# Attention with six score banks dealt out anew, exponentials head by head, and row sums once per pair of heads

## The chip, the cores and the metric

One core of one Trainium2 chip runs the whole layer. The metric is device time in microseconds (us) of one execution.

## The reference

The layer is causal attention, a residual and a layer norm, then a routed feed-forward (32 experts, one expert for each token, a bound on tokens per expert), a residual and a layer norm. The change is in the attention, and in where the work that follows a batch's attention is placed. Shapes: 8 batches of 1024 tokens, width 256, 16 heads of 64, keys and values from a latent of width 64, all float32.

```python
q_blhd = jnp.einsum('bld,dhk->blhk', x_bld, Wq)
latent_bll = jnp.einsum('bld,dc->blc', x_bld, Wkv_down)
k_blhd = jnp.einsum('blc,chk->blhk', latent_bll, Wk_up)
v_blhd = jnp.einsum('blc,chk->blhk', latent_bll, Wv_up)
attn = jnp.einsum('bqhd,bkhd->bhqk', q_blhd, k_blhd) / jnp.sqrt(HD)
attn = softmax(where(causal_mask, attn, neg_inf), axis=-1)
y_blhd = jnp.einsum('bhqk,bkhd->bqhd', attn, v_blhd)
out = jnp.einsum('bqhd,hdo->bqo', y_blhd, Wout)
x = _layernorm(x + out)
```

## The kernel before

**Pairs and slots.** Heads are taken two at a time: 8 batches of 8 pairs, 64 pairs; below, "pair p" is the place 0 to 7 in its batch. For each pair the kernel computes scores with keys on the partitions ("turned" scores) in 12 slots t (`NSLOT`, `SLOT`). Slots 0 to 3 are the first 512 queries against key blocks 0 to 3, slots 4 to 11 the second 512 queries against key blocks 0 to 7. The causal mask cuts the queries per head to 384 in slots 1 and 9, 256 in slots 2 and 10, and 128 in slots 3 and 11; the other six have 512.

**What a slot does.** TensorE (PE) forms the scores of both heads in `turned_scores`: for each head a product with the high parts (L669) and one with the low parts and the row maxima (L672). Slot n uses the two-bank tensor `turned_ps[n % 2]`, one bank per head. ScalarE (ACT) takes the exponential of both heads in one instruction (L928) into one of six buffers `probs`. GpSimd (POOL) clears what lies past the diagonal in slots 0 to 3 and 8 to 11 (`keep_past`, L451) and adds the exponentials up over the slots (`add_probs`, L466 to L475). PE multiplies the exponentials with the values (`values`, L692), two slots at a time, in the even slots: in slot t those of t-2 and t-1. ACT copies the result out (`copy_heads`).

**Row maxima.** The maxima for the next pair come from a second set of scores, with queries on the partitions: 24 units per pair, two in each slot (`row_scores`, L645), into two banks `row_ps`. VectorE (DVE) takes the maximum (`row_max`, L1078 and L1082). `turn_max` (L655) transposes them, `copy_max` (L1093) copies them out, and SyncE (SP) loads them into `q_max` with a DMA.

**Row sums.** `total` (L702) multiplies the added exponentials with ones, once for the first 512 queries (slot 6) and once for the second (slot 4 of the next pair). Each use has one product per head, and each product fills 64 rows of the bank. A float32 product is two instructions in the trace. DVE transposes the bank (`invert`, L1099), takes the reciprocal and transposes back (`invert_rows`, L1106 and L1111), and POOL divides the heads' outputs (`divide`, L483).

**The single bank `misc_ps`.** Everything else of PE goes through it, in the order of `LATE[gp, t]` (and `EARLY`, which runs between scores and row units): maxima to transpose, sums, queries of later pairs (`q`, L593), the output projection of the batch before (`proj`, L711), its transposes (`x1T`), router logits (`logits`) and the counts of places (`pos`). Each use waits until the one before was read. Every engine walks through the slots in the same order. In pairs 0 to 2 of a batch the batch before is projected, normalised and routed; POOL's part of the layer norm is `roots` (L489 to L501), and POOL sends the tokens away in pairs 4 and 5 (`send`, L508). Pairs 6 and 7 prepare the next batch. After the last pair comes `ENDING`, which finishes the last batch, and then the experts.

## Time and profile before

| what | us |
|---|---|
| median of three runs (2668.49 to 2669.42) | 2668.54 |
| profiled execution, its own time | 2669.0 |
| its span, first to last instruction | 2666.9 |
| PE busy | 2466.4 (92% of the span) |
| POOL busy | 1674.7 (63%) |
| DVE busy | 1532.1 (57%) |
| ACT busy | 994.5 (37%) |

The attention of the 64 pairs runs from 53.5 to 2327 us; the experts follow. Busy time is time in which an instruction runs, and matmuls overlap: the distance between the starts of two neighbours is what the first one costs. The mean granted TensorE clock is 0.968 of 2.4 GHz.

### The profile page before, as it was taken

To read this page: it belongs to the slowest core of one execution; us is meant where nothing else is said; L and a number is where in the kernel's file an instruction comes from. 1 tells how busy PE (TensorE), PEld (TensorE's weight loads), DVE (VectorE), ACT (ScalarE), POOL (GpSimd) and SP (SyncE) were. 2 spreads that over 40 slices of the span, in tenths; PEclk is the share of its full clock that TensorE was granted. 3 is DMA by queue.
4 is the path that set the end of the run, shared out by engine and by line. 5 is a ranking of instruction groups with operands and counts; after the bars stand their busy time and mean duration, and the time that the engine had idled before them with its cause. 6 is when DMAs were issued, how large, how long until landed. Compare 5 with 4: busy or idle time off the path is not lost.

```text
span 2666.9 us, 35643 instructions
## 1 busy us (share of the span) xinstructions
PE 2466.4 (92%) x12040; PEld 1578.6 (59%) x12040; DVE 1532.1 (57%) x4298; ACT 994.5 (37%) x1480; POOL 1674.7 (63%) x1623
## 2 busy tenths in 40 slices
PE   6999999999999999999999999999999999959995
PEld 5555665556655665566555655566556655646663
DVE  3666556665666556655666476656665666235453
ACT  3344424442444334433444244433443344212222
POOL 0677656865687657766686468665876678523343
PEclk7999999999999999999999999999999999969998
DMA  2122100200011001100020002000110011233552
GB/s 82 57 66 71 37 10 16 68 17 13 15 52 31 13 13 40 40 17 13 17 66 18 9 17 64 17 17 9 44 41 13 17 32 33 64 106 126 167 169 67
DMA packets 96804, 118.88 MB, mean 45 GB/s; under 512 B 12288, under 2 KB 75782, under 8 KB 96624
## 3 DMA queue, kind: packets, MB, share of 16 engines
q1 hardware_dynamic: 89712, 99.98, 13.4%
q0 software_dynamic: 6912, 16.64, 1.8%
q8 instruction: 97, 1.59, 0.3%
q14 instruction: 83, 0.68, 0.1%
HBM read 46.91 MB, written 37.90 MB: 32 GB/s over the span
## 4 chain that ended last, share of the span: by engine, by line
PE 62%; POOL 17%; issue 11%; DVE 6%; ACT 2%; DMA 1%; POOLq 0%; SPq 0%; ACTq 0%; DVEq 0%
PE value_ps L692 14%; POOL sums L475 10%; PE turned_ps L669 9%; PE row_ps L645 7%; PE turned_ps L672 7%; PE misc_ps L593 6%; PE misc_ps L711 4%; PE turned_ps L857 4%; PE misc_ps L702 4%; POOL probs L451 2%; POOL slots_x L508 2%; DVE masked_row L1078 1%; ACT probs L928 1%; PE misc_ps L876 1%; PE value_ps L876 1%
## 5 line engine op out<-in xcount | busy, mean ns | idle before, releaser
L928 ACT ACTIVATE probs<-turned_ps 128x1024 f32<-128x1024 f32 (+3 forms) x768 | 616.9, 811 | 961.2 <-PE turned_ps L672 953.1
L475 POOL TENSOR_TENSOR sums<-sums,probs 128x1024 f32<-128x1024 f32 (+3 forms) x512 | 830.6, 1622 | 23.1 <-ACT probs L928 14.7
L1078 DVE CUSTOM_DVE_ANT_0 masked_row<-row_ps,future 128x384 bf16<-128x384 f32 (+3 forms) x1024 | 464.4, 489 | 406.2 <-PE row_ps L645 405.1
L692 PE MATMUL value_ps<-probs,lat_keys 128*64 128x512 f32 (+3 forms) x3072 | 607.5, 508 | 44.8 <-POOL probs L451 41.2
L669 PE MATMUL turned_ps<-q_hl,lat_hi 128*128 128x512 f32 (+3 forms) x1536 | 570.3, 379 | 1.5 <-ACT fold_v L974 1.5
L672 PE MATMUL turned_ps<-q_max,lat_lo 65*128 65x512 f32 (+3 forms) x1536 | 528.4, 352 | 2.6 <-DMA q_max<-max_rows 2.6
L451 POOL TENSOR_SCALAR_AFFINE_SELECT probs<-probs 128x256 f32<-128x256 f32 x512 | 210.3, 411 | 500.3 <-ACT probs L928 499.6
L645 PE MATMUL row_ps<-lat_hi,q_hl 128*128 128x512 f32 (+3 forms) x1536 | 452.8, 366 | 14.3 <-DVE unit_max L1078 7.3
L471 POOL TENSOR_TENSOR sums<-probs 128x768 f32<-128x768 f32 (+1 forms) x128 | 268.5, 2097 | 233.0 <-ACT probs L928 233.0
L669 PEld LDWEIGHTS turned_ps<-q_hl,lat_hi 128*128 128x128 f32 x1536 | 294.2, 192 | 197.3 <-issue 149.0
L692 PEld LDWEIGHTS value_ps<-probs,lat_keys 128*64 128x64 f32 x3072 | 180.7, 137 | 348.5 <-issue 222.4
L1082 DVE TENSOR_REDUCE unit_max<-row_ps 128x1 f32<-128x512 f32 x512 | 327.9, 681 | 41.2 <-PE row_ps L645 36.4
L645 PEld LDWEIGHTS row_ps<-lat_hi,q_hl 128*128 128x128 f32 x1536 | 277.0, 193 | 91.2 <-DVE unit_max L1078 45.3
L672 PEld LDWEIGHTS turned_ps<-q_max,lat_lo 65*128 65x128 f32 x1536 | 295.4, 192 | 30.8 <-DMA q_max<-max_rows 2.9
L711 PE MATMUL misc_ps<-fold_v,headsT 128*128 128x256 f32 x1008 | 232.9, 384 | 2.4 <-POOL headsT L483 2.2
L711 PEld LDWEIGHTS misc_ps<-fold_v,headsT 128*128 128x128 f32 x1008 | 190.0, 192 | 35.1 <-issue 8.7
L1099 DVE STREAM_TRANSPOSE sums_cols<-misc_ps 128x512 f32<-128x512 f32 x127 | 91.1, 717 | 147.2 <-PE misc_ps L702 147.2
L483 POOL TENSOR_TENSOR headsT<-headsT,rinv_rows 128x512 f32<-128x512 f32 x128 | 164.2, 1283 | 1.9 <-DVE rinv_rows L1111 1.9
L910 ACT CAST q_hl<-misc_ps 64x512 fp32r<-64x512 f32 x125 | 72.6, 581 | 234.3 <-PE misc_ps L593 234.3
L857 PE MATMUL turned_ps<-ex_xT,ex_w 128*128 128x320 f32 x512 | 146.7, 440 | 0.0
L702 PE MATMUL misc_ps<-sums,ones_f 128*64 128x512 f32 x508 | 131.3, 595 | 7.7 <-DVE max_rows L1093 7.2
L1135 DVE TENSOR_TENSOR x<-misc_ps,x_in 128x256 f32<-128x256 f32 x64 | 27.2, 425 | 165.1 <-PE misc_ps L711 165.1
(187 smaller groups left out, 2317.4 us busy)
## 6 DMA issues: line engine op xcount, KB each, us to landing
q_max<-q_hl SPq DMA_DIRECT2D x256, 128.0 KB
slots_x<-zero_rows SPq DMA_DIRECT2D x8, 1290.0 KB, 6.4
ex_x<-slots_x SPq DMA_DIRECT2D x64, 129.0 KB, 3.5
x_in<-in_L_attn_x_bld SPq DMA_DIRECT2D x8, 1024.0 KB, 6.0
layer_out<-x_in SPq DMA_DIRECT2D x8, 1024.0 KB, 5.0
ex_w<-in_L_ffn_w_gate SPq DMA_DIRECT2D x32, 256.0 KB, 3.7
ex_w<-in_L_ffn_w_up SPq DMA_DIRECT2D x32, 256.0 KB, 3.8
ex_w<-in_L_ffn_w_down SPq DMA_DIRECT2D x32, 256.0 KB, 4.0
```

Source lines behind the costliest of these rows:

```text
L451: nc.gpsimd.affine_select(out=block, in_=block, pattern=[[0, 2], [1, P]], compare_op=ALU.is_ge, fill=0.0, base=0, channel_multiplier=-1).t ...
L471: nc.gpsimd.tensor_tensor(sums[c][:, :, q0:BANK], before[:, :, q0:BANK], now[:, :, q0:BANK], ALU.add).then_inc(added, 1)
L475: nc.gpsimd.tensor_tensor(sums[c][:, :, q0:BANK], sums[c][:, :, q0:BANK], now[:, :, q0:BANK], ALU.add).then_inc(added, 1)
L645: nc.tensor.matmul(dst[:, 0:k1 - k0], q_hl[gp % 2][:, h, i * P:(i + 1) * P], lat_hi[b % 2][:, k0:k1], start=True, stop=True).then_inc(rows ...
L669: nc.tensor.matmul(dst, lat_hi[b % 2][:, keys], q_hl[gp % 2][:, h, cols], start=True, stop=False)
L672: mm = nc.tensor.matmul(dst, lat_lo[b % 2][:, keys], q_max[:, c, h, q0:BANK], start=False, stop=True)
L692: mm = nc.tensor.matmul(value_ps[h * LD:(h + 1) * LD, q0:BANK], lat_keys[b % 2][:, j, :], probs[:, n % NPROBS, h, q0:BANK], start=(j == 0) ...
L711: mm = nc.tensor.matmul(bank[:, 0:D], headsT[:, (NPAIR * b + j) % NHEADS, i * P:(i + 1) * P], fold_v[:, j, :], start=(j == 0), stop=(j == ...
L857: mm = nc.tensor.matmul(turned_ps[f][:, m, 0:C], ex_w[e % AHEAD][:, m, kd, f * P:(f + 1) * P], ex_xT[:, g % 2, kd, u * C:(u + 1) * C], sta ...
L928: nc.scalar.activation(probs[:, n % NPROBS, :, q0:BANK], turned_ps[n % 2][:, :, q0:BANK], ACT.Exp).then_inc(exp_done, 1)
L1078: nc.vector.tensor_tensor_reduce(masked_row[n % 2][:, 0:width], row_ps[n % 2][:, 0:width], future[:, BANK - width:], scale=-1.0, scalar=-M ...
L1082: nc.vector.tensor_reduce(dst, row_ps[n % 2][:, 0:width], AX.X, ALU.max, negate=True).then_inc(max_done, 1)
```

## The change

- **Banks.** The six banks of the two kinds of scores are dealt out as three single banks for the turned scores (`SCORE_BANKS`) and three for the row units (`ROW_BANKS`).
- **Exponentials.** Each head's scores have a bank and an exponential of their own in the eight wide slots. In the narrow slots (2, 3, 10, 11) both heads share one bank, one product of each kind, and one exponential.
- **Row sums.** `sums` runs once per pair, in slot 4 of the next pair: four products (two heads, two halves of the queries), each filling 32 rows of the bank. DVE transposes the bank once, and in slots 6 and 8 takes the reciprocals of a half, with two small copies to fill all rows, and transposes them. There are three buffers of sums instead of two.
- **Order.** The maxima of the next pair's first half are transposed in slot 6 instead of within slot 4. `divide` moves to slots 7 and 0, and one half is divided a pair later. The projection, the layer norm and the routing of the batch before move to later slots. In the last pair all eight projections stand in slots 9 to 11.
- Some buffers share memory: `wkv2` with `sums_cols`, `zero_rows` with the router's.

`LAG` is 0, so the lines with it change nothing.

```diff
+        half_sums = [sb(f"half_sums{i}", [P, 2, BANK], F32, attn) for i in range(3)]
+        sums_of = lambda gp, c: half_sums[2 if c else gp % 2]
+        SCORE_BANKS = [turned_ps[0][:, 0, :], turned_ps[0][:, 1, :], turned_ps[1][:, 0, :]]
+        ROW_BANKS = [row_ps[0][:, :], row_ps[1][:, :], turned_ps[1][:, 1, :]]
+        BANKS_OF = [1 if 2 * (BANK - first_query(t)) <= BANK else 2 for t in range(NSLOT)]
...
             if gp + 1 < PAIRS:
                 late[1].append(("q", gp + 1, 1))
-                EARLY[gp, 4] = [("maxT", gp + 1, 0)]
+                late[6].append(("maxT", gp + 1, 0))
             if gp:
-                late[4].append(("sums", gp - 1, 1))
-            late[6].append(("sums", gp, 0))
+                late[4].append(("sums", gp - 1))
             if gp + 2 < PAIRS:
-                late[9 if p == NPAIR - 2 else 8].append(("q", gp + 2, 0))
+                late[9 if p == NPAIR - 2 else 7 if b and p < 2 else 8].append(("q", gp + 2, 0))
             if b and p == 0:
-                for i, t in enumerate((3, 5, 7, 10, 11)):
+                for i, t in enumerate((9, 10, 11)):
                     late[t].append(("proj", b - 1, i))
             if b and p == 1:
-                for i, t in enumerate((3, 5, 7)):
-                    late[t].append(("proj", b - 1, 5 + i))
-                for kd in range(KD):
-                    late[10 + kd].append(("x1T", b - 1, 0, kd))
+                for i, t in enumerate((3, 5, 9, 10, 11)):
+                    late[t].append(("proj", b - 1, 3 + i))
             if b and p == 2:
-                for kd in range(KD):
-                    late[3 + 2 * kd].append(("x1T", b - 1, 1, kd))
-                late[7].append(("logits", b - 1))
+                for use, t in zip([(hf, kd) for hf in range(2) for kd in range(KD)], (3, 5, 7, 10)):
+                    late[t].append(("x1T", b - 1, *use))
+                late[11].append(("logits", b - 1))
             if b and p == 3:
-                late[3].append(("pos", b - 1))
+                late[7].append(("pos", b - 1))
...
-        for t, i in zip((1, 2, 3, 5, 7, 8, 9, 10), range(NT)):
+        for t, i in zip((9, 9, 10, 10, 11, 11, 11, 11), range(NT)):
             LATE[PAIRS - 1, t].append(("proj", LAST, i))
...
POOL:
-                    if gp and t == 0:
+                    if gp >= 2 and t == 0:
+                        divide(gp - 2, 1)
+                    if gp and t == 7:
                         divide(gp - 1, 0)
-                    if gp and t == 6:
+                    if gp == PAIRS - 1 and t == 9:
                         divide(gp - 1, 1)
-                    if b and (p, t) in ((1, 0), (2, 0)):
+                    if b and (p, t) in ((1, 8), (2, 2)):
                         roots(b - 1, p - 1)
...
PE, row_scores:
                 if n >= 2:
-                    pe.wait_ge(max_done, n - 1)
+                    if n in ROW_BEFORE:
+                        pe.wait_ge(max_done, ROW_BEFORE[n] + 1)
-                dst = row_ps[n % 2]
+                dst = ROW_BANKS[row_bank(n)]
PE, turned_scores:
-                for h in range(2):
-                    dst = turned_ps[n % 2][:, h, q0:BANK]
-                    nc.tensor.matmul(dst, lat_hi[b % 2][:, keys], q_hl[gp % 2][:, h, cols], start=True, stop=False)
+                for h in range(BANKS_OF[t]):
+                    m = scored(n - 1) + h
+                    if m >= 3:
+                        pe.wait_ge(exp_done, m - 2)
+                    heads = slice(0, 2) if in_one_bank(t) else h
+                    nc.tensor.matmul(scores_of(n, h), lat_hi[b % 2][:, keys], q_hl[gp % 2][:, heads, cols], start=True, stop=False)
...
PE, total:
                 for h in range(2):
-                    mm = nc.tensor.matmul(bank[h * LD:(h + 1) * LD, :], ones_f[:, :], sums[c][:, h, :], start=True, stop=True)
+                    for c in range(2):
+                        k = 2 * h + c
+                        mm = nc.tensor.matmul(bank[k * 32:(k + 1) * 32, :], ones_f[:, :], sums_of(gp, c)[:, h, :],
+                                              start=True, stop=True)
ACT:
+                for h in range(BANKS_OF[t]):
+                    act.wait_ge(turned_full, scored(n - 1) + h + 1)
+                    heads = slice(0, 2) if in_one_bank(t) else h
+                    nc.scalar.activation(probs[:, n % NPROBS, heads, q0:BANK], scores_of(n, h), ACT.Exp).then_inc(exp_done, 1)
DVE:
+                for h in range(2):
+                    src, dst = (64 * h + 32 * k for k in (c, 1 - c))
+                    nc.vector.tensor_copy(rinv[dst:dst + 32, c, :], rinv[src:src + 32, c, :]).then_inc(inverse_done, 1)
...
+                    if gp and t in (6, 8):
+                        invert_rows(gp - 1, t // 8)
...
-                    if b and (p, t) in ((0, 11), (1, 8)):
-                        variance(b - 1, p)
-                    if b and (p, t) in ((1, 3), (2, 2)):
+                    if b and (p, t) in ((1, 5), (2, 0)):
+                        variance(b - 1, p - 1)
+                    if b and (p, t) in ((1, 10), (2, 4)):
                         normalise(b - 1, p - 1)
```

## Rows read from the trace of the kernel before

**Rows 1.** Windows: us, busy of each engine, granted clock, DMA share, GB/s.
```profile
216.00:245.50 29.50, 28.92 (x144) 17.17 (x143) 18.92 (x54) 13.12 (x18) 22.75 (x23) 1.00 0.22 64
684.80:722.90 38.10, 36.00 (x184) 22.91 (x183) 23.18 (x64) 14.71 (x22) 24.60 (x26) 0.91 0.07 15
...
407.00:412.00 5.00, 4.16 (x16) 3.08 (x17) 3.02 (x9) 0.97 (x2) 5.00 (x7) 0.69 0.23 52
```

**Rows 2.** Timeline of PE around the sums: start us, us busy, instruction, [idle before].
```profile
227.53 1.03 PE L702 MATMUL misc_ps<-sums,ones_f 128*64 128x512 f32 x4
228.48 0.50 PE L669 MATMUL turned_ps<-q_hl,lat_hi 128*128 128x512 f32 x1
...
230.68 0.64 PE L645 MATMUL row_ps<-lat_hi,q_hl 128*128 128x512 f32 x2
231.25 1.94 PE L692 MATMUL value_ps<-probs,lat_keys 128*64 128x512 f32 x8
233.01 1.03 PE L702 MATMUL misc_ps<-sums,ones_f 128*64 128x512 f32 x4
```

**Rows 3.** Timeline of PE in slots 2 to 4 of the same pair.
```profile
221.04 0.28 PE L669 MATMUL turned_ps<-q_hl,lat_hi 128*128 128x256 f32 x1
...
221.52 0.52 PE L645 MATMUL row_ps<-lat_hi,q_hl 128*128 128x384 f32 x2
...
223.62 0.33 PE L669 MATMUL turned_ps<-q_hl,lat_hi 128*128 128x128 f32 x1
...
224.12 0.67 PE L645 MATMUL row_ps<-lat_hi,q_hl 128*128 128x512 f32 x2
...
225.33 0.40 PE L672 MATMUL turned_ps<-q_max,lat_lo 65*128 65x512 f32 x1
226.07 0.27 PE L655 MATMUL misc_ps<-ident,neg_max 128*8 128x128 f32 x1 [0.33 <-DVE neg_max L1078]
...
226.82 0.87 PE L692 MATMUL value_ps<-probs,lat_keys 128*64 128x256 f32 x8
```

**Rows 4.** Timeline of PE in slot 10, and in slot 0 of the next pair.
```profile
241.53 0.28 PE L672 MATMUL turned_ps<-q_max,lat_lo 65*128 65x256 f32 x1
...
242.72 1.72 PE L692 MATMUL value_ps<-probs,lat_keys 128*64 128x512 f32 x8
...
246.33 0.22 PE L645 MATMUL row_ps<-lat_hi,q_hl 128*128 128x128 f32 x1
...
246.99 0.44 PE L692 MATMUL value_ps<-probs,lat_keys 128*64 128x256 f32 x2
```

**Rows 5.** Timeline of POOL from slot 9 of that pair to the next pair.
```profile
242.41 0.41 POOL L451 TENSOR_SCALAR_AFFINE_SELECT probs<-probs 128x256 f32<-128x256 f32 x1 [2.17 <-ACT probs L928]
...
247.25 0.41 POOL L451 TENSOR_SCALAR_AFFINE_SELECT probs<-probs 128x256 f32<-128x256 f32 x1
```

**Rows 6.** Timeline of ACT in slots 8 to 10 of that pair.
```profile
240.33 0.58 ACT L910 CAST q_hl<-misc_ps 64x512 fp32r<-64x512 f32 x1 [2.90 <-PE misc_ps L593]
...
241.53 1.30 ACT L928 ACTIVATE probs<-turned_ps 128x768 f32<-128x768 f32 x2
```

**Rows 7.** Groups of ACT by form: busy us, mean ns of one, idle before.
```profile
L928 ACT ACTIVATE probs<-turned_ps 128x1024 f32<-128x1024 f32 x384 | 393.2, 1024 | 657.4 <-PE turned_ps L672 653.2
...
L928 ACT ACTIVATE probs<-turned_ps 128x512 f32<-128x512 f32 x128 | 76.2, 595 | 12.9 <-PE turned_ps L672 11.3
```

**Rows 8.** Timeline of PE: pair 1, slot 2; pair 3, slot 4; pair 4, slot 4.
```profile
651.39 0.87 PE L692 MATMUL value_ps<-probs,lat_keys 128*64 128x384 f32 x4 [1.60 <-POOL probs L451]
...
450.88 0.65 PE L702 MATMUL misc_ps<-sums,ones_f 128*64 128x512 f32 x2 [1.01 <-DVE max_rows L1093]
...
767.57 0.44 PE L692 MATMUL value_ps<-probs,lat_keys 128*64 128x128 f32 x4 [0.69 <-POOL probs L451]
```

**Rows 9.** Timeline after the last pair: the sums, and the last division.
```profile
2329.11 1.08 PE L702 MATMUL row_ps<-sums,ones_f 128*64 128x512 f32 x4 [1.77 <-POOL sums L475]
...
2332.12 1.26 POOL L483 TENSOR_TENSOR headsT<-headsT,rinv_rows 128x512 f32<-128x512 f32 x1 [1.94 <-DVE rinv_rows L1111]
```

More of the change, by code:

```diff
@@ L245, in build_layer @@
         EARLY, LATE = {}, {}
-        last_sums = ("sums", PAIRS - 1, 1)
+        last_sums = ("sums", PAIRS - 1)
         for gp in range(PAIRS):
@@ L319, in wait_emptied, with scores_of @@
                 eng.wait_ge(misc_free, MISC[use] + 1)
+        in_one_bank = lambda t: 2 * (BANK - first_query(t)) <= BANK
+        def scores_of(n, h):
+            q0 = first_query(n % NSLOT)
+            bank = SCORE_BANKS[(scored(n - 1) + h) % 3]
+            if in_one_bank(n % NSLOT):
+                return bank[:, 0:2 * (BANK - q0)].rearrange("p (h q) -> p h q", h=2)
+            return bank[:, q0:BANK]
         def y_use(e, n):
@@ L818, in _ @@
                         row_scores(*unit)
-                    if t % VALUES == 0 and gp + t:
-                        values(gp * NSLOT + t - VALUES)
+                    if t % VALUES == LAG % VALUES and gp * NSLOT + t >= VALUES + LAG:
+                        values(gp * NSLOT + t - LAG - VALUES)
                     for use in LATE[gp, t]:
                         STAGES[use[0]](*use[1:])
-            values(PAIRS * NSLOT - VALUES)
+            for n0 in range(PAIRS * NSLOT - VALUES - LAG, PAIRS * NSLOT, VALUES):
+                values(n0)
             for use in ENDING:
@@ L989, in _ @@
                         pass_alone(b - 1, t)
-                    if b and (p, t) == (2, 10):
+                    if b and (p, t) == (3, 4):
                         gate_exponentials(b - 1)
@@ L1081, in row_max @@
                 else:
-                    nc.vector.tensor_reduce(dst, row_ps[n % 2][:, 0:width], AX.X, ALU.max, negate=True
+                    nc.vector.tensor_reduce(dst, row[:, 0:width], AX.X, ALU.max, negate=True
                                             ).then_inc(max_done, 1)
@@ L1164, in choose @@
                 use = ("logits", b)
+                if b == 0:
+                    dve.wait_ge(zeroed, 16 * NPAIR)
                 bank = wait_full(dve, use)
@@ L1260, in _ @@
                 if use[0] == "sums":
-                    invert_rows(*use[1:])
+                    for c in range(2):
+                        invert_rows(PAIRS - 1, c)
                 if use[0] == "rest" and use[2] == HPB - 1:
```

88 lines of the change are left out of this document (46 added, 42 removed).

## The prediction

> **What bounds the kernel now.** I read the page first: PE is busy 92% of the span, POOL 63%. The windows of single pairs come next. In a pair with nothing extra (215.92 to 245.40 us, 29.48 us long) PE is busy 28.92 us [rows 1], so PE's own order of starts sets the time, and only what shortens that order counts. The timeline of PE then tells what each piece costs and where it waits. Three things stand out in that pair: two visits to the sums, a wait for a row maximum in slot 4, and waits before row units in slots 10 and 0. Last I followed POOL and ACT through slots 8 to 0, to see who comes next when PE gets faster.
>
> **Sums.** A visit takes 0.95 us from its start to the next score product (227.53 to 228.48), of which about 0.1 is the change back to full-width products, which stays with the values ahead of it, so 0.86 each, 1.72 per pair [rows 2]. The visit is four instructions (two products, each in two) and two of them start together: the two heads stand in different 64 columns of the array. What four products of 32 columns cost no row shows. If all four run side by side, 0.86; if they pair up only where neighbours differ in head half, three steps, 1.29; if never more than two run at once, 1.72. To this comes one more change of column width. Such a change is seen between row units and values: 0.57 for two row units instead of 0.46, and 1.76 for eight instructions instead of 1.71 [rows 2], so 0.15. The gain per pair lies between 0.71 and a loss of 0.15. I take 0.5, between the first two cases, since two at once is seen to work in full: 64 x 0.5 = 32 us.
>
> **Narrow slots.** Four products of 128 columns take 0.50 in slot 3 (223.62 to 224.12) and four of 256 take 0.48 in slot 2, 0.12 each [rows 3]: 128 columns are no cheaper than about 0.11. Merged, slot 3 becomes two of 256, 0.24 and some 0.07 for the change of width at the start, 0.31: gain 0.19; slot 2 becomes two of 512 at 0.23: gain 0.01. Slots 10 and 11 are the same: 0.40 per pair. If a product over two heads' columns ran no faster than two, it would be 0.
>
> **Maxima out of slot 4.** From the last score product to the values 1.49 us pass, with a wait for DVE (225.33, 226.07, 226.82); without the transposition it is 0.23 and 0.57 [rows 3]: gain 0.69. In slot 6 it costs 0.03 to 0.05 behind the values, and the maxima are long there. Its bank is free: the sums' transposition on DVE ends two slots earlier. The DMA of the maxima, issued later by SP, still has slots 7 to 11, over 10 us, and SP has nothing urgent behind it. Gain 0.64 where the wait exists; in pairs 0 to 2 extra work already hides it, and 0.08 is left.
>
> **Third row bank.** In slot 10, 1.19 us pass from the last score product to the values (241.53 to 242.72), where 0.12 and 0.57 would do; in slot 0, 0.66 instead of 0.27 [rows 4]. Together 0.9, all waits for a maximum two units back; three units back is done in time. In slot 3 another 0.05.
>
> **What takes the place of that wait.** Here the gain is mostly lost. The values of slots 8 and 9 need the exponentials of slot 9, and these stand on ACT behind the two copies of the query (240.33, 241.53) [rows 6]. By head, 384 columns take an estimated 0.49 each (0.60 for 512, 1.02 for 1024 [rows 7], so 0.17 fixed), 0.98 instead of 0.81. So the values can start 2.5 us after slot 9 began (240.13) instead of 2.6. Behind the same exponential POOL starts `keep_past` at 242.41, adds slot 8, clears slot 10, adds slot 9, and clears slot 11 from 247.25 to 247.62 [rows 5]; the values of slot 11 wait for that already now, 0.2 to 0.3. That chain, 5.2 us of POOL's work in order, doesn't shrink and starts 0.17 later. PE would arrive 1.3 us earlier. In plain pairs all gains of slots 9 to 0 (0.9 of the banks, 0.2 of narrow slots) become wait, and 0.15 is lost. Where projections or logits stand in slots 9 to 11 (pairs 0 to 2), they cover the chain.
>
> **Exponentials by head.** 20 instead of 12 per pair, 0.17 each more, 1.4 us on an engine that is busy 13 of 29.5 [rows 1]: no cost elsewhere. With three banks the second head of slot 6 needs the first exponential of slot 5: product starts to exponential end about 1.4 us, wanted after 1.7. It fits.
>
> **Pairs with extra work.** Pairs 4 and 5: POOL sends tokens in slots 0 to 3, and the values of slot 3 wait for it (0.69 and more) [rows 8]. Narrow-slot and maxima gains before slot 4 vanish in this wait; 0.50 - 0.15 = 0.35 is left. Pair 1: `roots` on POOL holds up slot 2 by 1.8 us (1.60 idle [rows 8]); moved to slot 8 it lies beside projections: gain 1.8. Pair 2's `roots` moves from slot 0 to 2, and its wait from slot 2 to 4: I take no gain. There the clock falls too (0.69 in 407 to 412, 0.91 over pair 2 [rows 1]); I leave that as it is. Pair 3: the sums wait 1.01 behind the counts [rows 8], 1.2 with their start: gone.
> Last pair: eight projections in slots 9 to 11 follow each other through one bank, five waits of about 0.7 for DVE's addition: -3.5. After it, the first half's division no longer runs beside the sums: it follows them, with the sums (2329.11), transposition, reciprocal and transposition before the division at 2332.12 [rows 9]: -2.3. Work is only moved for `proj`, `x1T`, `logits` and `pos`. DVE trades one transposition (0.72) for four small copies, and is 64% busy. The setup and experts stay.
>
> **Sum.** Sums 32.0. Narrow slots 0.40 x 21 (pairs 0 to 2) + 0.20 x 27 (20 plain pairs and 7 pairs 6) = 13.8. Maxima 0.64 x 27 + 0.08 x 21 = 19.0. Row banks: (0.90 + 0.55 + 0.50) x 7 + 0.05 x 20 = 14.7, and 0.29 x 7 = 2.0 for the wait of slot 11 under pair 0's projections. Pair 1 12.6, pair 3 8.4. Longer exponential -0.15 x 34 = -5.1. End -5.8. Total 91.6. The profiled execution took 2669.0 (span 2666.9, 2.1 around it), so 2577; it is 0.5 above the median, which makes no difference here.
>
> **Rivals.**
> 1. POOL's chain does not bite: the wait at slot 11 is no more than today's. Then 34 pairs gain another 1.1 to 1.3, and the four products run side by side (+13): 2577 - 40 = 2535. For: POOL idles 2.2 us before 242.41 [rows 5]. Against: that idle time waits for the exponential, as above.
> 2. The four products never run more than two at once: -0.15 instead of +0.5 per pair, 64 x 0.65 = 42: 2619. With a narrow product without gain (14), 2633. Against: two do run at once.
> 3. The clock. Waits of 1.5 us in one place could make TensorE's clock fall as it does in pair 2 after its 2 us of waiting on POOL (0.69 of full in 5 us [rows 1]). A stretch of 6.8 us at half clock costs 3.4 us. At 34 plain pairs and pairs 4 and 5 that is 116 us: 2577 + 116 = 2693, slower than before. It decides from about 27 such falls on. Against: the wait is shorter than pair 2's, and pair 4's 0.7 causes none. A few falls, 10 of them, give 2611.
> 4. The sum is eaten elsewhere (bank waits of the three score banks, DVE): within 0.2% needs all 92 us gone. Little speaks for it.
>
> **Chances.** Forecast 0.55 (2555 to 2600), rival 1 0.15, rival 2 0.15, a few clock falls 0.07, rival 3 0.05, rival 4 0.03. The time is that of the forecast, 2577. The range 2535 to 2628 reaches to rival 1 and past the first form of rival 2. Within 0.2% (5.3 us) is what can't be told from no change. Faster 0.92, same 0.02, slower 0.06.
>
> **What would show it.** In a plain pair of the changed kernel: one group of eight L702-like instructions of 32 columns, 1.0 to 1.45 us; no gap in slot 4; two score products in slots 3 and 11, 0.3 us; no row unit waiting for DVE; and a PE wait of over 1 us for POOL's clearing before the values of slot 11, with the pair at 28.1 to 28.4 us. Pair 1 has no wait in slot 2, pair 2 one in slot 4. The granted clock in plain pairs stays 1.00. The forecast is wrong if that wait is missing (rival 1), if the sums take over 1.7 us (rival 2), or if the clock falls in plain pairs (rival 3).

## The result

Over four runs the changed kernel takes 2634.90 us in the median (2631.67 to 2638.45); the kernel before takes 2668.51. The ratio is 0.9878, its interval 0.9862 to 0.9894: 1.2% or 34 us faster, where 92 were forecast, and outside the forecast's range by 7. The profiled execution took 2635.0 us (span 2632.9), against 2669.0 before.

From the page of the changed kernel, its engines' busy time, and a group that matters below:

```profile
PE 2370.9 (90%) x11528; PEld 1518.4 (58%) x11528; DVE 1658.6 (63%) x4490; ACT 1030.6 (39%) x1992; POOL 1680.8 (64%) x1623
...
L1148 DVE COPY rinv<-rinv 32x16 f32<-32x16 f32 x256 | 171.6, 670 | 8.4
```

PE is busy 95.5 us less than before (2466.4 us), while the span is only 34.0 shorter: 61.5 us of new idle time stand against it. The window of one plain pair, with the columns of [rows 1]:

```profile
204.70:232.70 28.00, 26.88 (x136) 16.11 (x135) 21.04 (x57) 13.68 (x27) 22.86 (x22) 1.00 0.23 67
```

29.48 us have become 27.95, a little better than the 28.1 to 28.4 forecast. PE in slots 0 to 4 of that pair, in the order of the timeline ([rows 2, 3] are the same places before):

```profile
207.59 0.44 PE L720 MATMUL value_ps<-probs,lat_keys 128*64 128x128 f32 x4 [1.00 <-POOL probs L475]
...
212.96 0.39 PE L697 MATMUL turned_ps<-q_hl,lat_hi 128*128 128x256 f32 x1
...
213.30 0.64 PE L672 MATMUL row_ps<-lat_hi,q_hl 128*128 128x512 f32 x2
...
215.28 0.87 PE L720 MATMUL value_ps<-probs,lat_keys 128*64 128x256 f32 x8
216.08 1.07 PE L732 MATMUL misc_ps<-half_sums,ones_f 128*32 128x512 f32 x8
217.07 0.50 PE L697 MATMUL turned_ps<-q_hl,lat_hi 128*128 128x512 f32 x1
```

Four steps of the forecast can be read off. The wait before slot 11's values is there (1.00 in the line at 207.59, some 1.2 with what stands around it). Slot 3 has two narrow products in 0.34 us (212.96 to 213.30). Nothing stands between slot 4's row units and its values. And the sums take 0.99 us for eight instructions of 32 columns (216.08 to 217.07), where four of 64 columns took 0.95 [rows 2].

So the plain pairs did what they should. The loss is in the others. The table gives the length of a pair from the start of its first score product to that of the next pair's, read from the timelines; batches 1 to 7, mean of seven (pair 7: of six). "Forecast" is what the prediction's terms give for that pair, "came" what the two profiled executions differ by; the last column multiplies out. A second profiled execution of the changed kernel gives the same lengths within 0.5 us.

| pair | before | after | forecast gain | came | missing in all, us |
|---|---|---|---|---|---|
| 0 to 2 together | 126.11 | 122.65 | 6.98 | 3.46 | 24.7 |
| 3 | 31.42 | 31.57 | 2.44 | -0.15 | 18.1 |
| 4 and 5 together | 62.11 | 59.21 | 0.70 | 2.90 | -15.4 |
| 6 | 35.40 | 36.96 | 1.34 | -1.56 | 20.3 |
| 7 | 29.68 | 30.35 | 1.24 | -0.67 | 11.4 |
| batch 0 | 258.2 | 248.0 | 9.2 | 10.2 | -1.0 |
| last pair to the end | 391.9 | 396.7 | -5.3 | -4.8 | -0.5 |

The missing column adds up to 57.6 us, which is 91.6 less 34.0. Pairs 6 and 7 are even longer than before, though nothing of their extra work was touched.

Where they wait is in the view of PE's waits over the whole span (what waited, for what, us in total, times, longest):

```profile
PE value_ps L720 <- POOL probs L475: 64.3, 55, 1.9
...
PE misc_ps L645 <- DVE sums_cols L1135: 7.8, 7, 1.1
PE misc_ps L629 <- DVE sums_cols L1135: 7.8, 7, 1.1
PE misc_ps L742 <- DVE sums_cols L1135: 7.8, 7, 1.1
PE misc_ps L760 <- DVE sums_cols L1135: 7.5, 7, 1.1
```

The first line holds the forecast's wait for POOL's clearing. The other four were not forecast: four products of different kinds, once per batch each, wait 1.1 us for one and the same DVE instruction, `invert`, which transposes the sums out of the bank `misc_ps`. One of them in full, PE and DVE in pair 1, slot 5:

```profile
637.44 0.61 PE L732 MATMUL misc_ps<-half_sums,ones_f 128*32 128x512 f32 x4
637.98 0.50 PE L697 MATMUL turned_ps<-q_hl,lat_hi 128*128 128x512 f32 x1
...
639.51 0.29 DVE L1114 CUSTOM_DVE_ANT_0 masked_row<-turned_ps,future 128x128 bf16<-128x128 f32 x1
639.72 0.71 DVE L1135 STREAM_TRANSPOSE sums_cols<-misc_ps 128x512 f32<-128x512 f32 x1
...
640.49 0.70 PE L742 MATMUL misc_ps<-fold_v,headsT 128*128 128x256 f32 x2 [1.12 <-DVE sums_cols L1135]
```

The sums are in the bank by 638, but DVE's program has the transposition behind slot 5's row maxima, and so behind slot 5's row units on PE. It starts at 639.72, and slot 5's own use of the bank waits until it has ended.

This place in DVE's order is new. The section on the change does not name it, and its excerpt leaves these lines out (L1251 before, L1292 and L1296 after):

```diff
                             if use[0] == "sums":
-                                invert_rows(*use[1:])
+                                invert(*use[1:])
...
-                        if use[0] in STAGES and use[0] != "q":
+                        if use[0] in STAGES and use[0] not in ("q", "sums"):
```

In the kernel before, DVE did `invert` in the list of the sums' own slot, after that slot's row maxima, and only `invert_rows` behind the next slot's. In the pair of [rows 2] it starts at 228.60, as soon as PE has gone on to slot 5, and slot 5's row maxima follow at 229.78:

```profile
228.60 0.72 DVE L1099 STREAM_TRANSPOSE sums_cols<-misc_ps 128x512 f32<-128x512 f32 x1 [0.55 <-PE misc_ps L702]
```

The groups of the transposition, before and after, say the same for the whole kernel (at the end of each line stand the idle time before it and what ended it):

```profile
L1099 DVE STREAM_TRANSPOSE sums_cols<-misc_ps 128x512 f32<-128x512 f32 x127 | 91.1, 717 | 147.2 <-PE misc_ps L702 147.2
L1135 DVE STREAM_TRANSPOSE sums_cols<-misc_ps 128x512 f32<-128x512 f32 x63 | 44.8, 711 | 6.6 <-PE misc_ps L732 6.5
```

Before, DVE stood waiting for the sums in 113 of 127 cases; after, in 1 of 63. The bank is emptied late because the change moved the instruction that empties it, and the kernel before has no wait of PE for `sums_cols` in its list.

The second thing not forecast is on DVE. The reciprocals and the four small copies, DVE in slots 6 to 8 of the plain pair, and POOL beside them:

```profile
221.21 0.53 DVE L1148 COPY rinv<-rinv 32x16 f32<-32x16 f32 x2
...
225.58 0.24 DVE L1143 RECIPROCAL rinv<-sums_cols 128x16 f32<-128x16 f32 x1
225.86 2.37 DVE L1148 COPY rinv<-rinv 32x16 f32<-32x16 f32 x2
228.26 0.71 DVE L1152 STREAM_TRANSPOSE rinv_rows<-rinv 128x512 f32<-128x512 f32 x1
```
```profile
225.63 2.36 POOL L500 TENSOR_TENSOR half_sums<-half_sums,probs 128x1024 f32<-128x1024 f32 x1
```

A copy of 16 elements per lane takes 0.17 us in the median over the kernel (161 to 2203 ns for one). Here one waits until POOL's addition has ended, at 227.99, while the reciprocal before it ran into the same addition and took its usual 0.24. Counted over the trace, 127 of the 256 copies began while POOL was in an addition, a clearing or a division, and every one of them ended 23 to 32 ns after that instruction did; those that began with POOL idle, or beside an instruction of `roots`, took 161 to 172 ns. On this the Trainium skill ("SBUF — State Buffer", section "SBUF: two separate sides") says that VectorE and GpSimd share a pair of ports, that a float32 copy from SBUF to SBUF is among the VectorE operations that need it, and that whichever engine is second is blocked for the other's whole instruction; by this rule the trace agrees, with 2.2 us for a copy of 0.17. DVE's row maxima in the next slot come that much later, and in pairs 1, 2 and 6 something in slots 7 and 9 waits for DVE. The trace of the kernel before already had such a case: `variance` adds a constant to 128x4 numbers (L1150) in 0.17 us, but in slot 8 of pair 1 it took 2.03 us in each of the seven batches and ended with POOL's addition.

Third, the clock. Between the first and the last batch TensorE ran at half clock in 10 stretches of 51 us together before and in 20 of 89 us after, by the trace's clock record. The windows around one of them, batch 1's pair 7 in slots 5 and 6:

```profile
565.00:569.60 4.60, 3.48 (x27) 2.16 (x25) 1.91 (x7) 1.67 (x3) 2.45 (x3) 0.99 0.00 0
569.60:573.00 3.40, 3.40 (x10) 1.74 (x10) 1.91 (x5) 1.19 (x2) 2.19 (x2) 0.51 0.02 5
```

The slot-5 wait (PE busy 3.48 of 4.60 us) comes first, and then the granted clock is 0.51, so 1.2 GHz, for 3.4 us; slot 6 takes 5.04 us, where it takes 3.48 in experiment 1, without the wait.

Pair 3 shows two more costs of moved work. DVE handles the positions from slot 7 on instead of slot 3. There one of its instructions on 128x8 numbers, 0.17 us with POOL idle and 0.25 in pair 3 before, meets an addition in every batch and takes 2.28; slot 9's row maxima come late, and slot 10's row units wait for them. Then the clock falls. DVE, POOL and PE in slots 7 to 10 of batch 1, pair 3:

```profile
447.06 2.28 DVE L1243 SCALAR_TENSOR_TENSOR rt<-rt 128x8 f32<-128x8 f32 x1
```
```profile
446.93 2.38 POOL L500 TENSOR_TENSOR half_sums<-half_sums,probs 128x1024 f32<-128x1024 f32 x1
```
```profile
453.07 0.50 PE L672 MATMUL row_ps<-lat_hi,q_hl 128*128 128x512 f32 x1 [1.21 <-DVE unit_max L1114]
```

And the router's 32 products of 32 columns, now in pair 2's slot 11, are followed by half clock in pair 3's first slots:

```profile
422.80:429.60 6.80, 6.80 (x29) 5.59 (x29) 3.68 (x12) 2.41 (x5) 3.13 (x4) 0.50 0.00 0
```

Against a plain pair of batch 0, pair 3 is longer by 0.54, 0.55 and 1.89 us in slots 7, 9 and 10, and by 1.0 in slot 1 (means of seven batches).

### The profile page after: what moved, and what is told of

It reads as the page before. It is cut to its first block, busy times and chain, and to the rows that moved or that the text cites. A ratio compares the mean times of both kernels' runs of the same rounds, so it can differ in the third digit from the quotient of the medians.

```text
span 2632.9 us, 36668 instructions
## 1 busy us (share of the span) xinstructions
PE 2370.9 (90%) x11528; PEld 1518.4 (58%) x11528; DVE 1658.6 (63%) x4490; ACT 1030.6 (39%) x1992; POOL 1680.8 (64%) x1623
## 4 chain that ended last, share of the span: by engine, by line
PE 46%; POOL 25%; issue 15%; DVE 7%; ACT 2%; DMA 1%; POOLq 0%; SPq 0%; DVEq 0%; ACTq 0%
POOL half_sums L500 12%; PE value_ps L720 9%; PE turned_ps L697 6%; PE misc_ps L742 6%; PE turned_ps L700 5%; PE misc_ps L619 5%; POOL half_sums L495 4%; PE turned_ps L889 4%; PE row_ps L672 3%; POOL probs L475 3%; PE misc_ps L732 3%; POOL headsT L507 2%; POOL slots_x L532 2%; DVE unit_max L1118 2%; PE turned_ps L672 1%
## 5 line engine op out<-in xcount | busy, mean ns | idle before, releaser
L962 ACT ACTIVATE probs<-turned_ps 128x512 f32<-128x512 f32 (+2 forms) x1280 | 652.4, 553 | 800.5 <-PE turned_ps L700 785.5
L500 POOL TENSOR_TENSOR half_sums<-half_sums,probs 128x1024 f32<-128x1024 f32 (+3 forms) x512 | 829.7, 1621 | 56.1 <-ACT probs L962 41.8
L720 PE MATMUL value_ps<-probs,lat_keys 128*64 128x512 f32 (+3 forms) x3072 | 607.3, 511 | 68.8 <-POOL probs L475 64.3
L697 PE MATMUL turned_ps<-q_hl,lat_hi 128*128 128x512 f32 (+2 forms) x1280 | 536.0, 419 | 1.7 <-ACT fold_v L1007 1.7
L1114 DVE CUSTOM_DVE_ANT_0 masked_row<-row_ps,future 128x128 bf16<-128x128 f32 (+3 forms) x707 | 333.8, 492 | 264.0 <-PE row_ps L672 258.3
L700 PE MATMUL turned_ps<-q_max,lat_lo 65*128 65x512 f32 (+2 forms) x1280 | 486.5, 380 | 2.8 <-DMA q_max<-both_rows 2.8
L495 POOL TENSOR_TENSOR half_sums<-probs 128x768 f32<-128x768 f32 (+1 forms) x128 | 268.9, 2101 | 140.9 <-ACT probs L962 140.9
L672 PE MATMUL row_ps<-lat_hi,q_hl 128*128 128x512 f32 (+3 forms) x1026 | 320.1, 352 | 18.8 <-DVE unit_max L1114 10.1
L672 PE MATMUL turned_ps<-lat_hi,q_hl 128*128 128x512 f32 x510 | 177.7, 348 | 1.6 <-DVE unit_max L1118 1.6
L1114 DVE CUSTOM_DVE_ANT_0 masked_row<-turned_ps,future 128x256 bf16<-128x256 f32 (+1 forms) x317 | 149.7, 472 | 44.9 <-PE turned_ps L672 44.7
L1148 DVE COPY rinv<-rinv 32x16 f32<-32x16 f32 x256 | 171.6, 670 | 8.4
```

What stands on the lines that cost most here:

```text
L495: nc.gpsimd.tensor_tensor(sums_of(gp, c)[:, :, q0:BANK], before[:, :, q0:BANK], now[:, :, q0:BANK], ALU.add).then_inc(added, 1)
L500: nc.gpsimd.tensor_tensor(total, total, now[:, :, q0:BANK], ALU.add).then_inc(added, 1)
L672: nc.tensor.matmul(dst[:, 0:k1 - k0], q_hl[gp % 2][:, h, i * P:(i + 1) * P], lat_hi[b % 2][:, k0:k1], start=True, stop=True).then_inc(rows ...
L697: nc.tensor.matmul(scores_of(n, h), lat_hi[b % 2][:, keys], q_hl[gp % 2][:, heads, cols], start=True, stop=False)
L700: nc.tensor.matmul(scores_of(n, h), lat_lo[b % 2][:, keys], q_max[:, c, heads, q0:BANK], start=False, stop=True).then_inc(turned_full, 1)
L720: mm = nc.tensor.matmul(value_ps[h * LD:(h + 1) * LD, q0:BANK], lat_keys[b % 2][:, j, :], probs[:, n % NPROBS, h, q0:BANK], start=(j == 0) ...
```

## The experiments

Each is the changed kernel with the edit shown, timed in three rounds beside the kernel before on the same chip; ratios are to that kernel, with their 95% interval. The changed kernel itself, run again so: 2627.57 us, 0.9853 (0.9836 to 0.9869).

> The changed kernel as it is, on the chip of the next three, so that they can be compared with it: ratio to before 0.988 as in the first timing.

**1. The sums' bank is emptied one slot's maxima earlier.** DVE does `invert` at the end of slot 4's list instead of behind slot 5's row maxima. This is the place that it has in the kernel before.

```diff
                             if use[0] == "q":
                                 low_q(*use[1:])
-                            if use[0] == "sums":
-                                invert(*use[1:])
...
-                        if use[0] in STAGES and use[0] not in ("q", "sums"):
+                        if use[0] in STAGES and use[0] != "q":
```

> Changed kernel, but DVE transposes the sums' bank in slot 4 right after that slot's row maxima, instead of after the row maxima of slot 5. Theory A (the 58 us that are missing against the prediction lie in waits for the single bank of PE): the use of that bank in slot 5 (projection in pair 1, transposes in pairs 2 and 6, keys in pair 7) no longer waits some 1.2 us for DVE; slot 5 falls from 5.86 to about 4.7 us in pair 1 and from 2.90 to about 1.7 in pair 6; in all 25 to 34 us, 2601 to 2610. Rival B (the missing part is the clock and POOL alone): DVE's order costs nothing, at most 5 us change.

Measured: 2591.91 us, ratio 0.9703 (0.9675 to 0.9732). The same place in pair 1, DVE and PE:

```profile
627.37 0.72 DVE L1135 STREAM_TRANSPOSE sums_cols<-misc_ps 128x512 f32<-128x512 f32 x1 [0.72 <-PE misc_ps L732]
...
628.44 1.72 PE L742 MATMUL misc_ps<-fold_v,headsT 128*128 128x256 f32 x7
```

The transposition now waits for the sums and not for the maxima, and the projection has no wait. In batch 1 slot 5 is shorter by 1.33 us in pair 1, 1.31 in pair 6 and 1.19 in pair 7. The profiled span fell by 45.6 us, more than the 25 to 34 expected and the 30.9 of the four lines of waits. The clock gives more: 10 stretches of half clock with 34 us instead of 20 with 89, which is worth some 27 us (an estimate, half of the difference). Against it, slot 7 of pairs 2 and 6 and slot 8 of pair 7 became 0.7 to 0.8 us longer each, some 15 in all; experiment 5 shows that these belong to the copies. The same slots as above now read

```profile
556.00:560.60 4.60, 4.60 (x34) 2.97 (x30) 2.63 (x8) 2.18 (x5) 2.46 (x3) 1.00 0.03 6
560.60:564.00 3.40, 3.40 (x18) 1.60 (x17) 3.25 (x4) 1.01 (x3) 3.26 (x2) 1.00 0.02 5
```

Without the wait the clock stays. This one place in DVE's program cost more than half of the gain that was missing.

**2. No copies.** The swapped halves are written by reciprocals straight from the sums.

```diff
-                    nc.vector.tensor_copy(rinv[dst:dst + 32, c, :], rinv[src:src + 32, c, :]).then_inc(inverse_done, 1)
+                    nc.vector.reciprocal(rinv[dst:dst + 32, c, :], sums_cols[src:src + 32, :].rearrange("p (n q) -> p n q", q=32)[:, :, 0]
+                                         ).then_inc(inverse_done, 1)
```

> Changed kernel, but the two small copies of 32 x 16 reciprocals on DVE (0.17 us alone, 2.16 us beside an addition of POOL) are replaced by two reciprocals of the same size that read the sums again and write the other rows. Theory A: the copy is of a kind that has to wait until POOL's running instruction ends, the reciprocal is not: each takes about 0.17 to 0.25, DVE is 100 us less busy, and the waits for DVE in slots 7 and 9 of pairs 1 and 6 (0.8 us each) and in pair 3 go: 15 to 30 us, about 2612. Rival B: the long duration is a wait for a semaphore or for SBUF that any instruction there would have: no change in its duration, under 3 us.

Measured: 2610.07 us, ratio 0.9765 (0.9735 to 0.9795). The group, and the pair of instructions that stands for 225.86 above:

```profile
L1148 DVE RECIPROCAL rinv<-sums_cols 32x16 f32<-32x16 f32 x256 | 62.8, 245 | 8.3
```
```profile
225.88 0.52 DVE L1148 RECIPROCAL rinv<-sums_cols 32x16 f32<-32x16 f32 x2
```

Same place, same size, same addition on POOL beside it: 0.52 us instead of 2.37. In batch 1 slot 7 fell from 3.55 to 2.62 us in pair 1 and from 2.49 to 1.61 in pair 6, slot 9 of pair 6 from 4.03 to 3.21. It is the kind of operation that waits for POOL, not DVE's load. (The edit also changes what is read, `sums_cols` for `rinv`; both lie in SBUF, and the 0.17 us of the copies that meet no addition speak against `rinv` as the cause.) The plain pair stayed at 27.95: there the delay was hidden.

**3. Slot 11 is cleared before slot 9 is added.** This asks whether POOL's order sets the plain pair.

```diff
-                    if gp + t:
+                    if gp + t and t != NSLOT - 2:
+                        if t == NSLOT - 1:
+                            add_probs(gp, t - 2)
                         add_probs(*divmod(gp * NSLOT + t - 1, NSLOT))
```

> Changed kernel, but POOL clears slot 11 before it adds slot 9 (that addition of 1.8 us moves behind the clearing). If the POOL chain behind the exponential of slot 9 is what plain pairs wait for, as predicted: the wait of 1.23 us before the values of slot 11 goes, a plain pair falls from 27.95 to about 26.7 us, pair 0 and pair 5 to 7 by as much where they have it; about 30 pairs, 30 to 40 us, 2595 to 2605. Rival: the wait comes back at the next clearing (slots 0 and 1) since POOL's total is the same: under 10 us.

Measured: 2639.84 us, ratio 0.9883 (0.9852 to 0.9915): no difference from the changed kernel, so the rival came true. In the plain pair slot 0 fell from 3.27 to 2.03 us, all of the wait, but slot 2 rose from 2.56 to 3.33, and the pair ended at 27.50. The next thing in POOL's queue came late; POOL and PE in slots 1 and 2:

```profile
180.36 1.28 POOL L507 TENSOR_TENSOR headsT<-headsT,rinv_rows 128x512 f32<-128x512 f32 x1
181.59 0.41 POOL L475 TENSOR_SCALAR_AFFINE_SELECT probs<-probs 128x256 f32<-128x256 f32 x1
...
182.05 0.87 PE L722 MATMUL value_ps<-probs,lat_keys 128*64 128x384 f32 x4 [0.55 <-POOL probs L475]
```

The clearing of slot 1, which the values in slot 2 need, now stands behind the additions and the division. The wait moved by two slots, and what the plain pairs gained (0.45 us each) pair 4 lost (28.94 to 30.29).

**4. Two row banks again.** Only the third bank for the row maxima is taken back.

```diff
-        row_bank = lambda n: n % 2 if n < SETUP_UNITS else n % 3
+        row_bank = lambda n: n % 2
```

> Changed kernel, but the row units use two banks in turn again. If POOL's chain absorbs the gain of the third bank, as predicted: a plain pair stays within 0.2 us of 27.95, only pairs 0 to 2 lose about 0.5 each, under 12 us in all, up to 2647. Rival: the third bank is what the gain comes from: 0.9 us per plain pair and up, 40 to 60 us, 2675 or more.

Measured: 2649.88 us, ratio 0.9909 (0.9879 to 0.9939), against 0.9878 and 0.9853 for the two runs of the changed kernel. The interval overlaps that of the first of them, so the sign rests on the trace. There the plain pair is 28.21 instead of 27.95, a little outside the 0.2 us expected. The banks that remove 0.9 us of waits [rows 4] are worth 0.26 in a plain pair, and not where they were priced: slots 10 and 11 are 0.47 us longer without the third bank and slot 0, with the wait for POOL, 0.46 shorter, so that the gain there is taken as forecast. The 0.26 stand in slot 4 (3.55 instead of 3.30).

**5. Edits 1 and 2 together.**

> Changed kernel with both repairs on DVE: the sums' bank transposed in slot 4, and reciprocals in place of the two copies. Theory A (two separate sorts of waits for the single bank): the gains add, 0.953 to 0.960 of before, some 2548 to 2565 us; pair 1 at about 43.9 us, pair 6 at 35.5, plain pairs unchanged at 27.95. Rival: both gains are the same wait seen twice: no better than 0.970.

Measured: 2550.79 us, ratio 0.9564 (0.9548 to 0.9580). The two gains add, to slightly more than their sum (0.960): the slots that became longer in experiment 1 are now 1.61 and 1.56 us (slot 7 of pairs 2 and 6; 3.08 and 2.99 there) and 4.86 (slot 8 of pair 7; 5.61). Per pair, against the changed kernel: pair 1 43.92 (46.17), pair 2 34.65 (38.47), pair 6 34.17 (36.96), pair 7 27.56 (30.35), plain pair 27.95 (27.95). Pair 3 is not shorter (32.48, 31.57).

**6. Shorter additions.** Edits 1 and 2, and the row sums leave out all but 8 of the columns per head in slots 8 and 9. This computes less: its time is read as that of a POOL whose chain is 3.8 us shorter, and of no version of the kernel.

```diff
-                    total = sums_of(gp, c)[:, :, q0:BANK]
-                    nc.gpsimd.tensor_tensor(total, total, now[:, :, q0:BANK], ALU.add).then_inc(added, 1)
+                    short = t in (8, 9)
+                    total = sums_of(gp, c)[:, :, q0:q0 + 8 if short else BANK]
+                    nc.gpsimd.tensor_tensor(total, total, now[:, :, q0:q0 + 8 if short else BANK], ALU.add).then_inc(added, 1)
```

> As the kernel with both repairs on DVE, but POOL adds slots 8 and 9 over 8 queries instead of all (the row sums lack most of these two slots; 3.8 us less of POOL per pair). If POOL's work in order bounds the plain pair: the wait at slot 11 goes and does not come back, a plain pair takes 26.6 to 26.9 us instead of 27.95, pairs 4 and 5 gain too, in all 35 to 50 us against that kernel. Rival: the exponential of slot 9, late behind the query's copies, is the bound whatever POOL does: under 0.4 us per plain pair.

Measured: 2508.55 us, ratio 0.9409 (0.9394 to 0.9425), 42 us less than without this edit. The plain pair is 26.71 us. POOL in slots 9 to 11 there:

```profile
223.22 0.41 POOL L475 TENSOR_SCALAR_AFFINE_SELECT probs<-probs 128x256 f32<-128x256 f32 x1 [2.20 <-ACT probs L963]
223.59 0.22 POOL L501 TENSOR_TENSOR half_sums<-half_sums,probs 128x16 f32<-128x16 f32 x1
223.77 0.41 POOL L475 TENSOR_SCALAR_AFFINE_SELECT probs<-probs 128x256 f32<-128x256 f32 x1
224.15 0.22 POOL L501 TENSOR_TENSOR half_sums<-half_sums,probs 128x16 f32<-128x16 f32 x1
225.94 0.41 POOL L475 TENSOR_SCALAR_AFFINE_SELECT probs<-probs 128x256 f32<-128x256 f32 x1 [1.57 <-ACT probs L963]
```

With the additions gone from between them, the clearings wait for ACT and nobody waits for them. In the changed kernel the same five stand one behind the other:

```profile
230.21 0.41 POOL L475 TENSOR_SCALAR_AFFINE_SELECT probs<-probs 128x256 f32<-128x256 f32 x1 [2.22 <-ACT probs L962]
230.59 2.38 POOL L500 TENSOR_TENSOR half_sums<-half_sums,probs 128x1024 f32<-128x1024 f32 x1
232.91 0.41 POOL L475 TENSOR_SCALAR_AFFINE_SELECT probs<-probs 128x256 f32<-128x256 f32 x1
233.28 1.82 POOL L500 TENSOR_TENSOR half_sums<-half_sums,probs 128x768 f32<-128x768 f32 x1
235.06 0.40 POOL L475 TENSOR_SCALAR_AFFINE_SELECT probs<-probs 128x256 f32<-128x256 f32 x1
```

So 1.24 us of each plain pair is POOL's, and PE alone would need 26.7. This run takes work from POOL as well as from its chain; that the order is enough, with all of POOL's work (22.8 us in 26.7), experiment 7 shows.

**7. The order mended at both ends.** Edits 1 to 3, and the division of a pair's second half moves from slot 0 to slot 4.

```diff
-                    if gp >= 2 and t == 0:
+                    if gp >= 2 and t == 4:
                         divide(gp - 2, 1)
```

> As the kernel with both repairs on DVE, and of the orders on POOL only two: slot 11 is cleared before slot 9 is added, and the second half is divided in slot 4, where POOL idles, instead of slot 0. If the wait of 1.23 us moved to the clearing of slot 1 (as it did when only the clearing was put first) because a division of 1.3 us stood ahead of it: a plain pair falls to 26.7 us, about 25 us in all, 0.945 to 0.950 of before. Rival: POOL's total is the bound, nothing changes beyond 0.4 us per plain pair.

Measured: 2551.83 us, ratio 0.9560 (0.9538 to 0.9582), a miss: no faster than experiment 5. The plain pair came as expected, 26.71, and pair 6 fell to 32.95. But against experiment 5 pair 4 rose from 28.4 to 30.4, pair 5 stayed at 30.4, pair 2 rose from 34.7 to 37.4, and half clock stood in 32 stretches, 113 us. In pairs 4 and 5 the tokens are sent in slots 0 to 3, just where POOL now catches up.

**8. The sends, and pair 2's work, moved too.** (Run before experiments 7, 9 and 10, which take it apart.) With edit 7, tokens are sent in slots 4, 5 and 8 of pairs 4 to 6, pair 2's roots come in slot 4 and its normalisation in slot 6, with the transpositions behind it in 9 and 10.

```diff
-                for use, t in zip([(hf, kd) for hf in range(2) for kd in range(KD)], (3, 5, 7, 10)):
+                for use, t in zip([(hf, kd) for hf in range(2) for kd in range(KD)], (3, 5, 9, 10)):
...
-                    if b and (p, t) in ((1, 8), (2, 2)):
+                    if b and (p, t) in ((1, 8), (2, 4)):
...
-                    if b and p in (4, 5) and t < HPB:
-                        send(b - 1, (p - 4) * HPB + t)
+                    if b and p in (4, 5, 6) and t in (4, 5, 8) and (p - 4) * 3 + (4, 5, 8).index(t) < NT:
+                        send(b - 1, (p - 4) * 3 + (4, 5, 8).index(t))
...
-                    if b and (p, t) in ((1, 10), (2, 4)):
+                    if b and (p, t) in ((1, 10), (2, 6)):
```

> A version meant to be faster than both: both repairs on DVE, POOL clears slot 11 before it adds slot 9, the second half is divided in slot 4 instead of slot 0, tokens are sent in slots 4, 5 and 8 of pairs 4 to 6, the layer norm's roots of the second half stand in slot 4 of pair 2 with normalising in slot 6 and transposes in 9 and 10. If POOL's order and not its total is the bound, plain pairs fall to about 26.8 us and pairs 4 and 5 from 28.5 and 30.3 to 27 to 28: 30 to 50 us below the kernel with both repairs, 0.938 to 0.950 of before. Rival: POOL's total (23 us per pair and more) is so near that the waits come back elsewhere: within 10 us of it.

Measured: 2544.64 us, ratio 0.9546 (0.9526 to 0.9565), outside the range expected. Pairs 4 and 5 came down to 27.22 and 27.09, but pair 2 rose to 41.8, its slot 8 alone to 10.0 in batch 2. There, DVE, POOL and PE:

```profile
657.99 4.62 DVE L1199 TENSOR_SCALAR x<-x,mean_var,rstd 128x256 f32<-128x256 f32 x4
```
```profile
658.42 2.36 POOL L500 TENSOR_TENSOR half_sums<-half_sums,probs 128x1024 f32<-128x1024 f32 x1
```
```profile
663.01 0.50 PE L674 MATMUL turned_ps<-lat_hi,q_hl 128*128 128x512 f32 x1 [3.25 <-DVE unit_max L1116]
```

The four normalising instructions, about 0.41 us each elsewhere, take 4.62 beside POOL's addition and division (2.58 and 1.35 for the two that meet them), and the row maxima that PE needs stand behind them. This is the effect of experiment 2 in an operation of another kind.

**9. Only the sends moved.** Edit 7 and the sends of edit 8; pair 2's roots and normalisation where the changed kernel has them.

> As the kernel with all orders changed, but the roots and the normalising of pair 2 back in slots 2 and 4. In that kernel DVE's normalising stood beside POOL's additions in slot 6 and took 4.62 us for four instructions instead of 1.64, and pair 2 took 42.0 us. If that is the whole reason: pair 2 back at about 34 us, 50 us less than that kernel, 0.933 to 0.940 of before, about 2490. Rival: the other moves fill POOL so that pair 2 stays above 38 us.

Measured: 2537.51 us, ratio 0.9502 (0.9457 to 0.9547), a miss: the rival's pair 2 is what came. Pairs 4 and 5 stay at 27.24 and 27.11, so the sends are what brought them down. Pair 2 is 40.0: the normalisation in slot 4 now meets the division that was moved there and the two additions behind it (1.35, 2.54 and 2.56 us for the instructions that meet them), and in batch 1 its four instructions take 6.61 us.

```profile
384.84 6.61 DVE L1199 TENSOR_SCALAR x<-x,mean_var,rstd 128x256 f32<-128x256 f32 x4
```

**10. Roots in slot 4, normalisation in slot 5.** Experiment 9 and these two lines.

```diff
-                    if b and (p, t) in ((1, 8), (2, 2)):
+                    if b and (p, t) in ((1, 8), (2, 4)):
...
-                    if b and (p, t) in ((1, 10), (2, 4)):
+                    if b and (p, t) in ((1, 10), (2, 5)):
```

> As that, but pair 2's roots in slot 4 and the normalising in slot 5, where POOL adds nothing. If only the overlap with an addition makes DVE's instruction wait: the wait of 2 us for POOL's clearing in slot 4 of pair 2 goes too, pair 2 at 32 to 33 us, 8 to 14 us less than with the roots in slot 2, about 2480. Rival: DVE's normalising delays row maxima in slot 5 by as much: no difference.

Measured: 2482.74 us (2480.41 to 2486.81), ratio 0.9312 (0.9291 to 0.9333). It leaves no work out and beats both kernels. Pair 2 is 33.19 us; against experiment 9 its slot 4, where PE waited for POOL's clearing, is 2.1 us shorter, and slot 6, where it waited for DVE's row maxima, 3.9. A normalising instruction has its 0.41 us in the median again (0.58 in experiment 9), and the list of PE's waits has for POOL's clearing

```profile
PE value_ps L722 <- POOL probs L475: 4.9, 14, 1.7
```

instead of 64.3 us in 55 waits. The window of a plain pair:

```profile
200.00:226.70 26.70, 26.58 (x136) 16.13 (x135) 19.20 (x57) 13.59 (x27) 22.81 (x22) 1.00 0.24 71
```

PE is busy in 26.58 of 26.70 us: in such a pair nothing but PE's own work is left.

## Why the prediction was wrong

**The path was right.** PE's own order set the time, and every term that was read from rows of a plain pair held. The 20 plain pairs were to gain 1.24 each; in batch 0 they gained 1.53.

**Sums: right, undersized.** Four products of 32 columns run side by side in full, the case that gives 0.71. Measured are 0.73 (the 0.86 of the visit that is gone, less the 0.13 by which slot 4 grew from its values to the next score product: 1.66 us from 226.82 to 228.48 before, 1.79 from 215.28 to 217.07 after), where 0.5 was taken. That is 15 us more than forecast.

**Narrow slots, maxima, row banks, and the wait at slot 11: right.** 0.34 against 0.31 in slot 3; no gap in slot 4; the wait for POOL at 1.2 us and its cause by experiments 3, 4, 6 and 7. Rival 1 is out.

**Pairs 4 and 5: undersized.** 0.35 each was taken, since the earlier gains would vanish in the wait for the sends. They gained 2.20 and 0.70, 15 us more in all, of which 3 are those of the sums.

**"Its bank is free: the sums' transposition on DVE ends two slots earlier" failed.** This is the order of the kernel before. The change moved the transposition behind slot 5's row maxima, where in the plain pair shown it starts at 218.81, after slot 5's score products and row units on PE. For the maxima in slot 6 that is still early enough, and there the prediction stopped. But `misc_ps` is one bank with a queue of users, and slot 5 has one in pairs 1, 2, 6 and 7. The forecast put no price on this bank, and rival 4, which names bank waits and DVE, had "little speaks for it". Experiment 1, which only puts the instruction back to its old place, shows a cost of 1.7% of the kernel before (0.9866, the mean of the changed kernel's two ratios, to 0.9703), about 44 us. The waits themselves are 31 of them; the clock adds to that, and the copies took a part of it back.

**"DVE trades one transposition for four small copies" failed.** Their price was put at nothing because DVE was busy 18.9 of 29.5 us [rows 1]. By count and duration alone that holds: 256 copies of 0.17 us would be 44 us on DVE. They took 171.6, because each that meets a POOL addition waits for its end, and POOL is busy 23 of 28 us. Experiment 2 gives 1.0% of the kernel before (0.9866 to 0.9765), some 27 us. Both together are worth more than the sum, 3.0% or 81 us (0.9866 to 0.9564).

**"Work is only moved" failed in pairs 2 and 3.** The positions, moved to slot 7, now have an instruction that meets a POOL addition (2.28 us instead of 0.25) and hold up slot 10 of pair 3, and the router's narrow products are followed by half clock at the start of pair 3. Pair 3 misses 18 us in the table, and experiment 5 didn't shorten it (in its trace the same instruction takes 2.28 us again), so these two are the likely cause, by the slots the positions more than the clock. No run moved them back alone.

**The clock.** "I leave that as it is" and the rival of falls in the plain pairs both missed: plain pairs kept 1.00. There are 10 stretches more instead, and the ones looked at stand behind an unforeseen wait or the narrow products. At half clock 38 us more cost about 19 us (an estimate, half of it), inside the amounts above.

With the first two mended the change is worth 4.4% (experiment 5), more than the 3.4% forecast. By the trace the gains were undersized by about 27 us, while the two costs put at nothing were about 70 one by one (81 together) and pair 3 some 18. With 92 forecast this leaves 31 or 20 where 34 were measured, so the account closes to some 14 us at worst.

**Left open.** Why half clock stood in 32 stretches in experiment 7 and in 8 in experiment 10 with the same plain pair; the windows only show waits or narrow products ahead of the stretches that were looked at. The roots and the normalisation of pair 2 were moved in one run, so what each gave is read from slots alone. Pair 3's two causes were not tried apart.

## What to carry to other kernels

Read the change in every engine's order, not only in the order of the engine that it is for: one moved line on a half idle engine released a shared bank a slot later and cost more than half of the missing gain. For each bank that several users share, walk down all its users before and after, and look where in its own engine's order the instruction stands that frees it. A small instruction on a half idle engine is free only if its kind doesn't wait for another engine; look for the longest duration of operations of that kind in the trace, not the median (the kernel before had a 0.17 us instruction that took 2.03), and move such operations out of the other engine's busy stretches. And where an engine works in order, put the short work that others wait for ahead of the long work that nobody needs yet, at both ends of the stretch: mending one end only moves the wait.

## What the runs showed of the hardware that was not expected

- A float32 copy of 32x16 from SBUF to SBUF takes 0.17 us, up to 2.2 beside a POOL addition; a reciprocal of the same shape at the same place takes 0.245 on average over 256, with no such delay. The normalising operation with two scalars per lane (128x256) waits too: 0.41 us alone, 2.6 at the longest in experiment 8. So does an operation of 128x8 with two tensors in SBUF: 0.17 alone, 2.28 beside an addition.
- Four float32 products of 32 columns and 512 streamed columns run side by side in different 32 columns of the array: 0.99 us for all eight instructions and the change back to full width, against 0.95 for two products (four instructions) of 64 columns.
- One wait of 1.1 us with PE busy 3.48 of 4.60 us before it was followed by 3.4 us at half clock, and the same work without the wait was not.
